# A four-layer decoder on one core: three cross-attentions project queries before context keys, and two memsets in the layer-2 self-attention wait for the first normalised tiles

## The chip, the cores and the metric

The kernel runs on one core of one Trainium2 chip. The metric is the time of one execution on the device in microseconds, as the median of three runs. Six instruction queues work side by side and meet through semaphores: TensorE (PE, whose weight loads are listed as PEld), VectorE (DVE), ScalarE (ACT), GpSimd (POOL) and SyncE (SP), which here only issues transfers.

## What is computed

The reference is a decoder of four layers on `x` of 4 sequences, 512 tokens and 256 features, in float32. Each layer is `x += attention(layernorm(x))`, `x += cross_attention(layernorm(x), ctx)`, `x += ffn(layernorm(x))`, each of a kind of its own. The change touches four of the twelve stages. The three cross-attentions (layers 1, 2 and 3) have one form:

```python
x   = layer_norm(x, ...)              # here ctx, 64 rows a sequence
lat = layer_norm(latents, ...)        # here the 512 tokens
q = lat @ Wq
kv = concatenate([x, lat], axis=1) @ Wkv
k, v = split(kv, 2, axis=-1)
# layers 2 and 3: q and k are scaled to unit (rms or l2) rows, head by head
dots = einsum('bhid,bhjd->bhij', q, k) * scale
out = einsum('bhij,bhjd->bhid', softmax(dots), v) @ Wout
```

There are 16 heads of 64 in layers 1 and 2, and 8 heads of 64 in layer 3; layers 2 and 3 also mask context keys. The self-attention of layer 2 is a masked softmax attention with 16 heads of 16.

## The kernel before

The residual `k.x` stays in SBUF for the whole program (16 tiles of 128 tokens). Each stage is a function with a block of its own, in which each engine's instructions are written out by hand, in order, with semaphore waits. Between two stages all engines meet in a barrier, so a stage's weights are loaded and its first tiles normalised before TensorE has anything to do there. There is no scheduler: the order in the source is the order on each engine.

**Cross-attention** (`latent_attention`, called by `l1_xattn`, `l2_xattn`, `l3_xattn`; `unit` is set for layers 2 and 3). Ahead of the first batch's attention stand these steps:

- SP loads the context rows, small rows, then `Wkv`, `Wq` and the output weights (L2287 to L2293).
- DVE: statistics of the four token tiles of batch 0, two memsets, statistics of the context (L2826, L2829), `batch_scale` of the four token tiles (L2726), the scaled context `cn` (L2834), and for `unit` two operations on the mask. POOL computes the inverse deviations of tokens (L2644, L2647) and of the context (L2685, L2687).
- PE: `turn_batch` twice (L2338, four transposes each, both through bank 7, so the second waits until ACT has taken the first), eight small transposes of the context (L2465), then the projection "units" through the ring of banks 7, 0, 1, 2.
- ACT: `batch_gain` twice (L2534), then the context copied with gain and offset into `ctx2` (twice, L2599) and for `unit` into `ctxT` (L2603).

A unit is one projection of 512 features by two matmuls over the 256 inputs. The first `N0` units are context keys: 8 in layer 1 (256 columns), 4 in layer 2, 2 in layer 3 (512 columns). `NQ` units per batch follow for queries and token keys: 16, 16 and 8. In layer 1 ACT and DVE take turns in copying a unit out. With `unit`, each goes through a pipeline: `project` on PE (L2369), square on ACT, sum over 64 on DVE (L2748), a small scaling with a floor (L2751), the power -0.5 on POOL (L2667), the scaling on DVE (L2758), and `turn_unit` on PE three steps later (L2390). The trace records two matmul passes for each float32 matmul, so a unit is four records. Only when all units of batch 0 are placed does the first score follow (L2493).

**Layer-2 self-attention** (`l2_attn`). At its start DVE makes statistics of four tiles (L2034, L2041), POOL the inverse deviations (L1994, L1996), and then POOL fills `neg_max` and `values_and_ones` with three memsets (L2015, L2016, L2018). DVE scales the four tiles (L2048), PE transposes them (L1807), and the first key and query units follow (L1814). The memsets are first wanted by the first row maximum (`ones_set` 1) and by the first value unit (`ones_set` 3).

## Time and profile before

| | us |
|---|---|
| three runs | 3913.72, 3920.90, 3924.44 |
| median | 3920.9 |
| profiled execution, whole | 3895.01 |
| its span | 3893.3 |

The busy shares of the span are PE 89%, DVE 56%, ACT 39%, POOL 36%. The stages touched start at 605 us (layer-1 cross-attention), 1566 us (layer-2 self-attention), 1946 us (layer-2 cross-attention) and 3125 us (layer-3 cross-attention) of the span. In a timeline a row is a start, a length, the engine, the line, what is written from what, how many instructions, and in brackets how long the engine was idle before and what released it. The granted TensorE clock is 1.00 at 2.4 GHz and 0.50 at 1.2 GHz.

### The profile page before, as it was taken

The numbers are of one execution on the slowest core, as the hardware profiler recorded it, in microseconds if no ns is written. First come the engines' busy times: TensorE is split into PE (matmuls) and PEld (weight loads), VectorE is DVE, ScalarE is ACT, GpSimd is POOL, SyncE is SP. The second block draws the span as 40 slices with busy tenths as digits, with TensorE's granted clock in tenths as the row PEclk, the third lists the DMA queues.
The fourth block names the chain that finished last, engine by engine and source line by source line (L and its number), as shares of the span: only waits on it lengthen the run. The fifth ranks groups of instructions, "written<-read, shape, count | busy, mean of one in ns | idle before, by whom it ended". The sixth has DMA issues, their size and how long they took to land. (4 is left out here: it accounts for less than half of the span.)

```text
span 3893.3 us, 54516 instructions
## 1 busy us (share of the span) xinstructions
PE 3471.5 (89%) x18930; PEld 2243.6 (58%) x18930; DVE 2192.1 (56%) x5349; ACT 1506.5 (39%) x3064; POOL 1392.1 (36%) x1928
## 2 busy tenths in 40 slices
PE   7998897999999978788888999999896979997996
PEld 5675684445555557344444555556794445555996
DVE  6374444646555558666367676765434456665454
ACT  2253102434434265133344444443453134443453
POOL 2141441423223245233244445443423134443412
PEclk9999978999999988899889999999898889997998
DMA  2005001000000000000010000000421000003312
GB/s 101 1 1 125 15 1 46 1 1 1 1 1 1 13 1 1 24 1 1 1 49 1 1 1 1 1 1 1 165 90 60 1 29 1 1 1 112 126 57 83
DMA packets 48720, 108.86 MB, mean 28 GB/s; under 512 B 6660, under 2 KB 32900, under 8 KB 46404
## 3 DMA queue, kind: packets, MB, share of 16 engines
q1 hardware_dynamic: 40964, 84.88, 6.6%
q0 software_dynamic: 7488, 20.49, 1.5%
q8 instruction: 158, 2.59, 0.3%
q14 instruction: 110, 0.90, 0.1%
HBM read 70.67 MB, written 34.68 MB: 27 GB/s over the span
## 5 line engine op out<-in xcount | busy, mean ns | idle before, releaser
L2655 POOL TENSOR_SCALAR probs<-probs,inv_sum 128x512 f32<-128x512 f32 x640 | 438.2, 698 | 997.2 <-DVE inv_sum L2776 996.9
L2618 ACT ACTIVATE probs<-psum_banks,neg_max 128x576 f32<-128x576 f32 x640 | 468.5, 737 | 733.2 <-DVE neg_max L2861 733.2
L2861 DVE TENSOR_REDUCE neg_max<-psum_banks 128x1 f32<-128x576 f32 x640 | 455.0, 752 | 209.4 <-PE psum_banks L2493 202.8
L2493 PE MATMUL psum_banks<-keys_T,queries_T 64*128 64x288 f32 x2560 | 405.7, 436 | 52.5 <-ACT probs L2618 43.2
L2785 DVE COPY probs_T<-psum_banks 128x512 f32<-128x512 f32 x640 | 409.0, 680 | 4.2 <-PE psum_banks L2411 4.2
L2493 PEld LDWEIGHTS psum_banks<-keys_T,queries_T 64*128 64x128 f32 x2560 | 223.8, 189 | 268.8 <-ACT probs L2618 147.7
L2411 PE MATMUL psum_banks<-ident,probs 128*128 128x128 f32 x2560 | 357.6, 284 | 3.3 <-POOL probs L2655 2.4
L2411 PEld LDWEIGHTS psum_banks<-ident,probs 128*128 128x128 f32 x2560 | 281.2, 143 | 129.2 <-POOL probs L2655 75.2
L2443 PE MATMUL psum_banks<-probs_T,values 128*64 128x512 f32 x1280 | 311.3, 608 | 2.2 <-issue 2.2
L4419 PE MATMUL psum_banks<-sorted_T,tile_weights 128*128 128x128 f32 x2208 | 266.9, 278 | 0.0
L4419 PEld LDWEIGHTS psum_banks<-sorted_T,tile_weights 128*128 128x128 f32 x2208 | 259.5, 195 | 0.1
L2857 DVE TENSOR_TENSOR psum_banks<-psum_banks,key_mask 128x128 f32<-128x128 f32 x192 | 57.5, 299 | 273.3 <-PE psum_banks L2493 273.3
L2667 POOL TENSOR_TENSOR square_sum<-square_sum,neg_half 128x8 f32<-128x8 f32 x102 | 167.0, 1639 | 69.8 <-DVE square_sum L2751 68.3
L4318 POOL DMA_INDIRECT expert_outputs<-expert_rows,output_index x92 | 89.7, 975 | 268.6 <-DVE expert_rows L4703 115.8
L4435 PE MATMUL psum_banks<-w_L_experts_down,hidden_T 128*128 x736 | 174.3, 380 | 2.2 <-DVE expert_rows L4703 1.4
L2346 PE MATMUL psum_banks<-w_L_xattn_Wkv,batch_normed_T 128*128 128x512 f32 x320 | 156.3, 612 | 0.0
L2443 PEld LDWEIGHTS psum_banks<-probs_T,values 128*64 128x64 f32 x1280 | 78.9, 137 | 134.0 <-issue 123.2
L4500 ACT COPY tile_weights<-w_L_experts_up 128x1024 f32 (+1 forms) x92 | 135.3, 1472 | 22.9 <-issue 22.9
L4435 PEld LDWEIGHTS psum_banks<-w_L_experts_down,hidden_T 128*128 128x128 f32 x736 | 132.8, 190 | 17.2 <-issue 2.9
L1962 ACT ACTIVATE probs_T<-psum_banks 128x512 f32<-128x512 f32 (+3 forms) x128 | 83.0, 701 | 127.4 <-PE psum_banks L1899 126.5
L2658 POOL TENSOR_TENSOR context_probs<-probs,inv_sum 128x128 f32<-128x128 f32 x320 | 128.7, 402 | 0.0
L2618 ACT ACTIVATION_READ_ACCUMULATOR probs<-psum_banks,neg_max 128x1 f32 x640 | 125.4, 196 | 0.0
(538 smaller groups left out, 6160.1 us busy)
## 6 DMA issues: line engine op xcount, KB each, us to landing
normed<-sorted_rows SPq DMA_DIRECT2D x30, 385.5 KB, 3.4
sorted_rows<-zero_rows SPq DMA_DIRECT2D x8, 1028.0 KB, 16.6
w_L_experts_down<-in_L_experts_down SPq DMA_DIRECT2D x2, 4096.0 KB, 20.4
normed<-expert_outputs SPq DMA_DIRECT2D x8, 1024.0 KB, 6.9
w_L_xattn_Wkv<-in_L_xattn_Wkv SPq DMA_DIRECT2D x2, 2048.0 KB, 8.3
w_L_experts_up<-in_L_experts_up SPq DMA_DIRECT2D x1, 4096.0 KB, 12.2
sorted_rows<-zero_rows SPq DMA_DIRECT2D x4, 899.5 KB, 15.9
x_res<-in_x SPq DMA_DIRECT2D x4, 512.0 KB, 6.7
```

What stands on the lines that cost most here:

```text
L2346: last = pe.matmul(k.ps[:, 7, :], rows, wkv[:, c, W + a * 512:W + (a + 1) * 512], start=c == 0, stop=c == KC - 1)
L2411: last = pe.transpose(k.ps[:, 4 + n % 2, c * P:(c + 1) * P], prob[:, (b * NS + s) % PB, at + c * P:at + (c + 1) * P], k.ident[:, :])
L2443: last = pe.matmul(k.ps[r, 6, :], values[:, b % VB, c, (2 * j + h) * 64:(2 * j + h + 1) * 64], pT[:, q % 2, h, c, :], start=c == 0, stop=F ...
L2493: last = pe.matmul(k.ps[:, 2 * h + a, 0:HALF], qT[r, b % 2, j, t * P:(t + 1) * P], kT[r, j, k0:k0 + HALF], start=True, stop=True)
L2618: act.activation(prob[:, g % PB, h * w:(h + 1) * w].rearrange("p (a n) -> p a n", a=2), k.ps[:, 2 * h:2 * h + 2, 0:HALF], ACT.Exp, bias=nm ...
L2655: pool.tensor_scalar(w, w, inv[:, g % 4, h:h + 1], 1.0, ALU.mult, ALU.mult).then_inc(shared, 1)
L2667: pool.tensor_tensor(ss[:, i % 4, 2, :], ss[:, i % 4, 1, :], k.half[:, 0:8], ALU.pow).then_inc(inverted, 1)
L2785: dve.tensor_copy(pT[:, q % 2, h, :, t * P:(t + 1) * P], k.ps[:, 4 + n % 2, :].rearrange("p (c q) -> p c q", q=P)).then_inc(copied, 1)
L2861: dve.tensor_reduce(nmax[:, g % 4, h:h + 1], k.ps[:, 2 * h:2 * h + 2, 0:HALF], AX.XY, ALU.max, negate=True).then_inc(maxed, 1)
L4419: last = pe.matmul(ps[:, 2 * (n % 2) + part, f * P:(f + 1) * P], wt[:, n % 2, c, part * 512 + f * P:part * 512 + (f + 1) * P], xsT[:, n % ...
L4435: last = pe.matmul(ps[:, 6, 0:D], h[:, n % 2, f * P:(f + 1) * P], w_down[:, f // F, f % F * D:f % F * D + (E - 1) * STEP + D][:, bass.ds(a ...
L4500: act.copy(wt[:, n % 2, :, :], w_up[:, :, 0:(E - 1) * STEP + UP][:, :, bass.ds(at, UP)]).then_inc(weights_copied, 1)
```

## The change

In the three cross-attentions the first four units are now units of batch 0 (`AHEAD` = 4); the `N0` context units follow, and then the rest. The context transposes stand behind the third unit. The second `turn_batch` of batch 0 goes through bank 0, with no wait for ACT between the two. DVE scales the token tiles ahead of the context's statistics, and the context rows behind step 0; the mask operations stand behind step 3. ACT fills `ctxT` (or, in layer 1, the first copy of `ctx2`) at step 3, and the rest of `ctx2` later. SP loads `Wq` first, then the key half of `Wkv` with a semaphore of its own, then the value half. In the layer-2 self-attention POOL waits for the four scaled tiles before its memsets. No operation is dropped or added, apart from one more transfer a stage, since `Wkv` comes in two.

```diff
                 batch_rstd(0)
+                pool.wait_ge(normed, TT)
                 pool.memset(top[:, :, :], 0.0).then_inc(ones_set, 1)
...
+    AHEAD = 4
+    CONTEXT_TURN = 3
+    CONTEXT_COPY = AHEAD + N0 + 1
...
+        def is_context(i):
+            return AHEAD <= i < AHEAD + N0
+
+        def unit_place(i):
+            return (0, i) if i < AHEAD else ((i - N0) // NQ, (i - N0) % NQ)
...
-                sp.dma_start(wkv[:, :, :], wkv.src[:, :, :]).then_inc(kv_loaded, 16)
                 sp.dma_start(wq[:, :, :], wq.src[:, :, :]).then_inc(q_loaded, 16)
+                sp.dma_start(wkv[:, :, 0:W], wkv.src[:, :, 0:W]).then_inc(keys_loaded, 16)
+                sp.dma_start(wkv[:, :, W:2 * W], wkv.src[:, :, W:2 * W]).then_inc(kv_loaded, 16)
...
                 turn_batch(0, 0)
-                pe.wait_ge(norm_moved, 1)
-                turn_batch(0, 1)
+                turn_batch(0, 1, 0)
+                pe.wait_ge(norm_moved, KC)
+                pe.wait_ge(q_loaded, 16)
+                if not unit:
+                    pe.wait_ge(keys_loaded, 16)
+                for i in range(CONTEXT_TURN):
+                    step(i, 0, units_before(1))
                 pe.wait_ge(ctx_normed, B)
...
-                pe.wait_ge(norm_moved, KC)
+                for i in range(CONTEXT_TURN, units_before(1) + 3):
+                    if i == AHEAD:
+                        pe.wait_ge(ctx_ready, KC)
+                        pe.wait_ge(keys_loaded, 16)
+                    step(i, 0, units_before(1))
                 pe.wait_ge(ctx_ready, (3 if unit else 2) * KC)
                 pe.wait_ge(kv_loaded, 16)
-                for i in range(N0):
-                    step(i, 0, units_before(1))
-                pe.wait_ge(q_loaded, 16)
-                for i in range(N0, units_before(1) + 3):
-                    step(i, 0, units_before(1))
...
                 for i in range(units_before(1) + 3):
+                    if i == CONTEXT_TURN:
+                        for c in range(KC):
+                            act.wait_ge(ctx_turned, c + 1)
+                            if unit:
+                                act.activation(ctxT[:, c, :], k.ps[:, 4 + c, 0:B * NC], ACT.Identity,
...
+                            else:
+                                context_rows(c, 0)
+                    if CONTEXT_COPY <= i < CONTEXT_COPY + KC:
+                        if unit:
+                            context_rows(i - CONTEXT_COPY, 0)
+                        context_rows(i - CONTEXT_COPY, 1)
                     step(i, 0, units_before(1))
...
+                for t in range(TT):
+                    batch_scale(0, t)
                 dve.wait_ge(ctx_loaded, 16)
...
-                for t in range(TT):
-                    batch_scale(0, t)
+                step(0, 0, units_before(1))
                 dve.wait_ge(ctx_rstd, 1)
...
+                for i in range(1, AHEAD):
+                    step(i, 0, units_before(1))
```

On PE at the start of the layer-1 cross-attention there stood, from the token transposes on (rows of the program's order, in which a count is of matmuls):

```order
L2338 MATMUL psum_banks<-ident,batch_normed 128x128 x8
L2465 MATMUL psum_banks<-ident,probs_T 128x64 x8
L2377 MATMUL psum_banks<-context_T_twice,w_L_xattn_Wkv 128x256 x16
L2381 MATMUL psum_banks<-batch_normed_T,w_L_xattn_Wq 128x512 x2
L2381 MATMUL psum_banks<-batch_normed_T,w_L_xattn_Wkv 128x512 x2
```

Now there stands, on the same engine and from the same place (line numbers are those of the changed file):

```order
L2349 MATMUL psum_banks<-ident,batch_normed 128x128 x8
L2393 MATMUL psum_banks<-batch_normed_T,w_L_xattn_Wq 128x512 x2
L2393 MATMUL psum_banks<-batch_normed_T,w_L_xattn_Wkv 128x512 x2
L2393 MATMUL psum_banks<-batch_normed_T,w_L_xattn_Wq 128x512 x2
L2482 MATMUL psum_banks<-ident,probs_T 128x64 x8
L2393 MATMUL psum_banks<-batch_normed_T,w_L_xattn_Wkv 128x512 x2
L2389 MATMUL psum_banks<-context_T_twice,w_L_xattn_Wkv 128x256 x16
```

Three units moved ahead of the context transposes, and one more ahead of the context keys.

On DVE at the start of the layer-2 cross-attention there stood (`probs_T` holds the context rows here):

```order
L2823 MEMSET context_values 64x512 x2
L2826 BN_STATS context_stat<-probs_T 64x6 x4
L2829 BN_AGGR context_mv<-context_stat 64x2 x4
L2726 TENSOR_SCALAR batch_normed<-x_res,batch_mv,batch_rstd 128x256 x4
L2834 TENSOR_SCALAR probs_T<-probs_T,context_mv,context_rstd 64x256 x4
L2839 TENSOR_SCALAR key_mask<-w_mask_bf 128x256
L2841 TENSOR_SCALAR key_mask<-key_mask 128x256
L2748 TENSOR_REDUCE square_sum<-squares 128x8
L2751 TENSOR_SCALAR square_sum<-square_sum 128x8
```

Now there stands:

```order
L2848 MEMSET context_values 64x512 x2
L2751 TENSOR_SCALAR batch_normed<-x_res,batch_mv,batch_rstd 128x256 x4
L2853 BN_STATS context_stat<-probs_T 64x6 x4
L2856 BN_AGGR context_mv<-context_stat 64x2 x4
L2773 TENSOR_REDUCE square_sum<-squares 128x8
L2776 TENSOR_SCALAR square_sum<-square_sum 128x8
L2860 TENSOR_SCALAR probs_T<-probs_T,context_mv,context_rstd 64x256 x4
L2773 TENSOR_REDUCE square_sum<-squares 128x8
L2776 TENSOR_SCALAR square_sum<-square_sum 128x8
```

The token tiles are scaled before the context is looked at, and the scaled context moved behind the first unit's square sum.

## Rows read from the trace of the kernel before

**Rows 1.** The page: busy time and share of each engine

```profile
PE 3471.5 (89%) x18930; PEld 2243.6 (58%) x18930; DVE 2192.1 (56%) x5349; ACT 1506.5 (39%) x3064; POOL 1392.1 (36%) x1928
```

**Rows 2.** Timeline, start of the layer-1 cross-attention, all engines

```profile
605.82 0.57 SPq L2291 DMA_DIRECT2D w_L_xattn_Wkv<-in_L_xattn_Wkv  x1
...
607.44 1.01 POOL L2647 TENSOR_TENSOR batch_rstd<-batch_rstd,neg_half 128x4 f32<-128x4 f32 x1
...
608.83 1.40 DVE L2826 BATCH_NORM_STATS2 context_stat<-probs_T 64x6 f32<-64x256 f32 x4 [0.46 <-DMA probs_T<-in_ctx_rows]
...
610.56 1.34 DVE L2726 TENSOR_SCALAR batch_normed<-x_res,batch_mv,batch_rstd 128x256 f32<-128x256 f32 x4
...
611.95 1.11 PE L2338 MATMUL psum_banks<-ident,batch_normed 128*128 128x128 f32 x4 [13.55 <-DVE batch_normed L2726]
...
613.94 1.12 PE L2338 MATMUL psum_banks<-ident,batch_normed 128*128 128x128 f32 x4 [0.87 <-ACT batch_normed_T L2534]
...
614.98 1.11 PE L2465 MATMUL psum_banks<-ident,probs_T 64*128 64x64 f32 x8
...
615.77 1.92 ACT L2599 ACTIVATE context_T_twice<-psum_banks,feature_vectors 128x256 f32<-128x256 f32 x4
...
617.79 9.30 PE L2377 MATMUL psum_banks<-context_T_twice,w_L_xattn_Wkv 128*128 128x256 f32 x32 [1.69 <-issue]
```

**Rows 3.** Transfers in 600 to 640 us: size, us to landing

```profile
w_L_xattn_Wkv<-in_L_xattn_Wkv SPq DMA_DIRECT2D x1, 2048.0 KB, 8.1
```

**Rows 4.** Timeline, start of the layer-2 cross-attention, all engines

```profile
1948.32 0.43 SPq L2291 DMA_DIRECT2D w_L_xattn_Wkv<-in_L_xattn_Wkv  x1
...
1948.93 1.02 POOL L2647 TENSOR_TENSOR batch_rstd<-batch_rstd,neg_half 128x4 f32<-128x4 f32 x1
...
1953.44 1.11 PE L2338 MATMUL psum_banks<-ident,batch_normed 128*128 128x128 f32 x4 [8.92 <-DVE batch_normed L2726]
...
1960.19 8.80 PE L2369 MATMUL psum_banks<-w_L_xattn_Wkv,probs_T 128*128 128x512 f32 x16 [2.61 <-issue]
```

**Rows 5.** Transfers in 1940 to 1975 us: size, us to landing

```profile
w_L_xattn_Wkv<-in_L_xattn_Wkv SPq DMA_DIRECT2D x1, 2048.0 KB, 8.5
```

**Rows 6.** Timeline, start of the layer-3 cross-attention, PE

```profile
3138.49 6.71 PE L2369 MATMUL psum_banks<-w_L_xattn_Wkv,probs_T 128*128 128x512 f32 x8 [2.61 <-issue]
```

**Rows 7.** Timeline, start of the layer-2 self-attention, all engines

```profile
1568.84 1.01 POOL L1996 TENSOR_TENSOR token_rstd<-token_rstd,neg_half 128x4 f32<-128x4 f32 x1
...
1569.80 1.80 POOL L2015 MEMSET neg_max<- 128x2048 f32 x1
1569.96 6.28 DVE L2048 TENSOR_SCALAR batch_normed<-x_res,token_mv,token_rstd 128x256 f32<-128x256 f32 x4 [1.49 <-POOL token_rstd L1996]
...
1576.30 1.97 PE L1807 MATMUL psum_banks<-ident,batch_normed 128*128 128x128 f32 x8 [11.65 <-DVE batch_normed L2048]
...
1579.03 3.75 PE L1814 MATMUL psum_banks<-batch_normed_T,w_L_padded_Wk 128*128 128x512 f32 x4 [0.77 <-ACT batch_normed_T L1951]
```

**Rows 8.** Durations of single lines: ns min/median/max, first and last start

```profile
L2048 DVE TENSOR_SCALAR batch_normed<-x_res,token_mv,token_rstd x16: 396/406/5237, 1570.0 to 1767.6; 128x256 f32<-128x256 f32 x16
...
L2751 DVE TENSOR_SCALAR square_sum<-square_sum x102: 171/171/206, 1965.3 to 3453.6; 128x8 f32<-128x8 f32 x102
...
L2685 POOL TENSOR_SCALAR context_rstd<-context_mv x3: 1230/1232/1232, 610.7 to 3130.5; 64x4 f32<-64x4 f32 x3
...
L2644 POOL TENSOR_SCALAR batch_rstd<-batch_mv x12: 194/194/195, 607.2 to 3409.7; 128x4 f32<-128x4 f32 x12
```

**Rows 9.** Windows: stretch, its length, busy time of each engine, granted clock, DMA

```profile
618.00:622.10 4.10, 4.10 (x10) 3.25 (x11) 0.42 (x1) 0.37 (x1) 0.00 (x0) 0.50 0.01 2
...
1566.00:1946.00 380.00, 314.61 (x2144) 157.15 (x2144) 218.50 (x392) 116.42 (x184) 109.58 (x283) 0.89 0.02 7
...
1576.30:1584.70 8.40, 7.63 (x15) 4.09 (x16) 0.00 (x0) 1.86 (x3) 0.00 (x0) 0.50 0.00 0
...
1960.10:1963.60 3.50, 3.41 (x4) 1.50 (x5) 0.00 (x0) 0.00 (x0) 0.00 (x0) 0.50 0.14 56
```

More of the change, by code:

```diff
@@ L2332, in bank_free, with turn_batch @@
                                 pe.wait_ge(ctx_value_moved, b * A + A)
-                def turn_batch(b, c):
+                def turn_batch(b, c, bank=7):
                     if c == 0:
@@ L2337, in turn_batch @@
                     for t in range(TT):
-                        last = pe.transpose(k.ps[:, 7, t * P:(t + 1) * P], xr[:, t, c * P:(c + 1) * P], k.ident[:, :])
+                        last = pe.transpose(k.ps[:, bank, t * P:(t + 1) * P], xr[:, t, c * P:(c + 1) * P], k.ident[:, :])
                     last.then_inc(norm_turned, 1)
@@ L2375, in project @@
                     for c in range(KC):
[L2376 to L2377 removed]
+                        if is_context(i):
+                            j = i - AHEAD
+                            last = pe.matmul(k.ps[:, unit_bank(i), 0:B * NC], wkv[:, c, j * P:(j + 1) * P],
                                              ctx2[:, c, :, 0, :], start=c == 0, stop=c == KC - 1)
                         else:
[L2380 removed]
+                            j, w = unit_place(i)[1] // 2, (wkv if i % 2 else wq)
                             last = pe.matmul(k.ps[:, unit_bank(i), :], w[:, c, j * P:(j + 1) * P], xT[:, c, :],
@@ L2533, in batch_gain @@
                     act.wait_ge(norm_turned, KC * b + c + 1)
-                    act.activation(xT[:, c, :], k.ps[:, 7, :], ACT.Identity, bias=k.vec(pre + lb)[:, c:c + 1],
+                    bank = 0 if b == 0 and c == 1 else 7
+                    act.activation(xT[:, c, :], k.ps[:, bank, :], ACT.Identity, bias=k.vec(pre + lb)[:, c:c + 1],
                                    scale=k.vec(pre + lg)[:, c:c + 1]).then_inc(norm_moved, 1)
@@ L2540, in project @@
                     act.wait_ge(made, i + 1)
-                    if i < N0:
-                        act.copy(kc[:, i, :, :].rearrange("p b n -> p (b n)"),
+                    if is_context(i):
+                        act.copy(kc[:, i - AHEAD, :, :].rearrange("p b n -> p (b n)"),
                                  k.ps[:, unit_bank(i), 0:B * NC]).then_inc(act_moved, 1)
                     else:
-                        b, j = (i - N0) // NQ, (i - N0) % NQ // 2
+                        b, j = unit_place(i)[0], unit_place(i)[1] // 2
                         act.mul(qT[:, b % 2, j, :], k.ps[:, unit_bank(i), :], 0.125).then_inc(act_moved, 1)
@@ L2563, in step, with context_rows @@
                                 gain).then_inc(moved, 1)
+                def context_rows(c, i):
+                    act.activation(ctx2[:, c, :, i, :], k.ps[:, 4 + c, 0:B * NC].rearrange(
+                        "p (b n) -> p b n", b=B), ACT.Identity, bias=k.vec(pre + cb)[:, c:c + 1],
+                        scale=k.vec(pre + cg)[:, c:c + 1]).then_inc(ctx_ready, 1)
                 def copy_ctx(b, j):
@@ L2595, in _ @@
                     batch_gain(0, c)
-                for c in range(KC):
-                    act.wait_ge(ctx_turned, c + 1)
-                    for i in range(2):
-                        act.activation(ctx2[:, c, :, i, :], k.ps[:, 4 + c, 0:B * NC].rearrange(
-                            "p (b n) -> p b n", b=B), ACT.Identity, bias=k.vec(pre + cb)[:, c:c + 1],
-                            scale=k.vec(pre + cg)[:, c:c + 1]).then_inc(ctx_ready, 1)
-                    if unit:
-                        act.activation(ctxT[:, c, :], k.ps[:, 4 + c, 0:B * NC], ACT.Identity,
-                                       bias=k.vec(pre + cb)[:, c:c + 1],
-                                       scale=k.vec(pre + cg)[:, c:c + 1]).then_inc(ctx_ready, 1)
-                for i in range(units_before(1) + 3):
+                for i in range(units_before(1) + 3):
+                    if i == CONTEXT_TURN:
[3 more added lines that the diff above has]
+                                act.activation(ctxT[:, c, :], k.ps[:, 4 + c, 0:B * NC], ACT.Identity,
+                                               bias=k.vec(pre + cb)[:, c:c + 1],
+                                               scale=k.vec(pre + cg)[:, c:c + 1]).then_inc(ctx_ready, 1)
+                            else:
[4 more added lines that the diff above has]
+                        context_rows(i - CONTEXT_COPY, 1)
                     step(i, 0, units_before(1))
@@ L2764, in place @@
                     if unit:
-                        dve.wait_ge(moved, N0)
+                        dve.wait_ge(moved, AHEAD + N0)
                     else:
-                        dve.wait_ge(act_moved, N0 // 2)
-                        dve.wait_ge(dve_moved, N0 // 2)
+                        dve.wait_ge(act_moved, (AHEAD + N0) // 2)
+                        dve.wait_ge(dve_moved, (AHEAD + N0) // 2)
                     if b:
@@ L2842, in _ @@
                     dve.wait_ge(mask_made, 2)
-                for i in range(units_before(1) + 1):
+                for i in range(AHEAD, units_before(1) + 1):
                     step(i, 0, units_before(1))
```

19 lines of the change are left out of this document (8 added, 11 removed).

## The prediction

> **What bounds the kernel now.** The page comes first: PE is busy 89% of the span, DVE 56%, and no other engine is near [rows 1]. Such a share is an average over twelve stages, and the change touches only the first microseconds of four of them, so I read the timelines of those starts. Because a barrier stands ahead of each stage, nothing can overlap its start, and a microsecond saved there ends the stage a microsecond earlier, provided that PE's queue is what the stage then runs on. In these starts PE is the engine that waits. Before the token transposes it is idle for 13.55 us in layer 1, 8.92 us in the layer-2 cross-attention and 11.65 us in the layer-2 self-attention, each time released by DVE's scaled tiles [rows 2, 4, 7]; part of this is the end of the stage before. It is idle again, 1.69, 2.61 and 2.61 us, before the first context unit [rows 2, 4, 6].
>
> What the reader is to see in [rows 2] is the order of causes. POOL has the tokens' inverse deviation at 607.44 + 1.01 = 608.45. DVE could scale the tiles then, but its queue has the context's statistics first (608.83), and it scales at 610.56. PE turns tile half 0 at 611.95, waits 0.87 us for ACT to empty bank 7, turns the second half, then the context (1.11 us). Now ACT needs four copies of the context (1.92 us from 615.77), and only after them does the first unit start, at 617.79. The queries need none of the context's work.
>
> **The token scaling, moved ahead.** In the self-attention the scales start 0.11 us after POOL's power has ended (1569.85 to 1569.96) [rows 7]; so in layer 1 they start at 608.56, take their 1.34 us [rows 2], and PE begins at 609.95 instead of 611.95. In the layer-2 cross-attention the power ends at 1949.95 [rows 4], so PE begins at 1951.45 instead of 1953.44. The context statistics then run beside PE's transposes.
>
> **Two banks for the two turns.** Two turns of 1.11 us back to back and then ACT's last copy, of the size of the 0.87 us wait: 2.22 + 0.87 = 3.1 us. PE is ready for the first unit at 613.05 in layer 1, 1954.55 in layer 2.
>
> **The loads.** Layer 1 needs `Wq` and the key half of `Wkv`, together the same 2 MB that `Wkv` had alone. Those were issued at 605.82 and landed 8.1 us later [rows 2, 3], so at 613.9; with one more issue in between I take 614.0. The weights are thus the last to arrive there, by 0.9 us. In layer 2 the first unit needs only `Wq`, 1 MB. The 2 MB of `Wkv`, from 1948.32, took 8.5 us [rows 4, 5]: half the size lands between half of that (1952.6) and all of it (1956.8). I take 1954.55, where PE is ready, since the middle of the two is 1954.7; the late end would cost 2.2 us. The same holds in layer 3 with half the bytes. The key half in layers 2 and 3 has four units of time to land, and the value half is wanted only after all units: nothing.
>
> **The units.** The first one starts at 614.0 instead of 617.79: 3.8 us. In layer 2 it starts at 1954.55 instead of 1960.19: 5.6 us. Layer 3 shows the same 2.61 us of idle before its first context unit [rows 6] and the same code ahead of it; I take 5.5. From this goes what was ahead of the units and now stands among them: eight context transposes, 1.11 us at the half clock, 0.55 at the full clock that I expect behind the third unit. Results: **3.2, 5.1 and 5.0 us**. The number of units, their columns and the ring of banks are as before. ACT's copies of the context for the values move into the stream of units: 1.92 us for four, so 0.96 for each of two steps. A unit is 8.80 us for four, half of it at the lower clock [rows 4], some 1.8 us of PE, plus a turn; ACT has a square and a gain in that time and room for about 1 us. I cost them at 0, and at 0.5 us a stage if ACT is late. The mask's two DVE operations move likewise: 0, since PE turns a unit three steps after it projects it.
>
> **The memsets.** In [rows 7] DVE starts four scales at 1569.96, and they end at 1576.24. One of the sixteen scales of this stage took 5237 ns, the median is 406 [rows 8]; in the cross-attention, beside transfers at full load but no memset, four take 1.34 us. The one long scale lies under POOL's memsets, which began at 1569.80. With POOL waiting, the scales end at 1571.30 and PE starts at 1571.36 instead of 1576.30: **4.9 us**. What is queued behind POOL's new wait is the memsets alone. They need about 5.5 us, so end near 1577. The key unit, moved from 1579.03 to about 1574.1, the query and the first score come before the first row maximum, and before any value unit; before, these stood past 1584 [rows 9]. So the wait itself costs 0. If the memsets blocked another DVE operation in their new place, at most the 4.9 us would be given back. Only 1 MB of weights is wanted for key and query, and the larger 2 MB of layer 1 landed in 8.1 us, so they are there.
>
> **Sum.** 3.2 + 4.9 + 5.1 + 5.0 = **18.2 us**. The profiled span of 3893.3 us would become 3875.1. The profiled execution lies 26 us under the median of the three runs, which scatter by 10.7 us, so I apply the difference to the median: 3920.9 - 18.2 = **3902.7**.
>
> **A rule against the change.** In layers 2 and 3 the four context scales on DVE (SBUF to SBUF) now stand right behind the square sum that releases POOL's power, some 1.6 us long. Rows show the conflict in two directions: the memset held a scale for 5.2 us, and `context_rstd` on POOL took 1230 ns, against 194 for its kin on the tokens, while DVE scaled tiles [rows 8]. The third row speaks against it for the power: the small scaling on DVE, which comes next to powers, never took over 206 ns. The Trainium skill, page "SBUF — State Buffer", section "Who interferes with whom", says that the one of VectorE (in a two-port mode) and GpSimd that issues first holds the shared ports for its whole instruction and the other is fully blocked. By it the context scales could come a whole power later.
>
> **Rivals.** (1) *The clock eats half of it.* All four starts run at 1.2 GHz: PEclk is 0.50 up to 622.1, 1584.7 and 1963.6 [rows 9]. If the clock rose at these same moments however early PE starts, the time gained would be worked at half rate: lost are half of 3.8, of 5.6, of 5.5 and of 4.9, about 10 us, and the result is 3912.8, within 0.3%. For it: the clock is no engine's queue. Against it: each rise came 3.4 to 5.7 us after PE had begun to work without a gap (617.79, 1960.19, 1579.03), whatever the stage; so it follows the work, and moves with it. (2) *The port is held.* A unit at half rate is 3.4 us, its square and sum I estimate at 1.7, the power at 1.6, then the four scales at 1.4: the context is ready 8.1 us after the first unit's start. PE arrives at 3.4 + 2 x 1.75 = 6.9 us if the clock rises early: a wait of 1.2 us, twice, so 3905.1. (3) *The memset is not the cause*, and the scales stay slow: 13.3 us, 3907.6. One long row and its start beside the memset speak against it. (4) *Slower.* The clock also falls and rises inside the layer-2 self-attention, 0.89 on average over 380 us, so 84 us at half rate [rows 9], where PE, DVE and POOL hand work to each other. All of this is now met at other moments. Each microsecond more at half rate costs up to half of one, so the gain is gone from 36 us more on; 48 us more would give 3927. Nothing in the change lengthens PE's gaps there, and three runs of one program differ by 10.7 us in all, so this is a tail.
>
> **How the numbers follow.** Forecast with all four terms 0.70, the clock 0.18, the port 0.05, the memset 0.04, slower 0.03. A measurement tells about 0.3% (11.8 us) from no change, so all but the clock and the tail would be faster by more. The forecast lies only 6 us beyond that bound, and the medians scatter by some microseconds each; I take faster 0.74, same 0.23, slower 0.03. The range goes down to 3891 (the clock rises earlier relative to the first unit, and scatter of the runs) and up to 3913, the clock rival.
>
> **What would show it.** In the changed profile PE's first token transpose comes 2.0 us earlier from each cross-attention's first DVE statistics, with no gap between the two turns; the first unit of layer 1 starts about 8.2 us after the issue of its first weights, waiting for a transfer. No scale in the self-attention is over 0.5 us. The first score comes 3, 5 and 5 us sooner in its stage. It is wrong if the rise of the clock stays where it was, if PE has a gap before the context transposes, or if the row maxima wait for a memset.

## The result, and the profile after

| | before, us | after, us |
|---|---|---|
| median of the runs | 3920.9 (5 runs, 3913.72 to 3924.44) | 3901.12 (5 runs, 3896.46 to 3907.86) |
| profiled execution, whole | 3895.01 | 3901.12 |
| its span | 3893.3 | 3899.4 |

The ratio is 0.9949, with a 95% interval of 0.9934 to 0.9964: 19.8 us faster, where 18.2 were forecast (3902.7). A second comparison, on a later occasion, gave 3900.14 against 3921.65 us, ratio 0.9942 (0.9929 to 0.9955). So the kernel is faster by about 0.5%.

The two profiled spans alone would say the opposite: 6.1 us slower. Whoever compares profiles has to look at the stages. Stage lengths, from the first transfer that SP issues in a stage to that of the next, in us. The third column is a second profile of the kernel before, taken beside the second comparison:

| stage | before | before, again | after |
|---|---|---|---|
| layer-1 cross-attention | 730.6 | 730.7 | 730.2 |
| layer-1 feed-forward (untouched) | 230.8 | 224.7 | 228.5 |
| layer-2 self-attention | 380.1 | 385.4 | 372.5 |
| layer-2 cross-attention | 782.4 | 783.0 | 779.1 |
| layer-2 experts and layer-3 self-attention (untouched) | 396.0 | 412.8 | 412.7 |
| layer-3 cross-attention | 439.9 | 440.2 | 432.7 |
| layer-3 experts (untouched) | 304.3 | 314.4 | 315.3 |

The four touched stages together went from 2333.0 to 2314.5: 18.5 us. What hides it are two stretches of untouched code, which in the first profile of before happened to be 16.7 and 11.0 us shorter than after, and which the same kernel shows long in its second profile. A second profile of the changed kernel has them long too (413.0 and 315.0), so only the first profile of before is short. Whether that is the execution, the chip or the occasion is not shown: 12 runs of this kernel on one chip lie within 17 us (3913.64 to 3930.48). By the two second profiles the four touched stages went from 2339.3 to 2317.5, 21.8 us. The windows of the first stretch say so, before, before again, and after (columns: stretch, its length, busy time and count of PE, PEld, DVE, ACT, POOL, granted clock, DMA share, GB/s):

```profile
2729.00:3125.00 396.00, 336.43 (x1744) 254.00 (x1744) 156.46 (x398) 135.98 (x223) 128.00 (x120) 0.86 0.23 78
```

```profile
2730.70:3143.50 412.80, 343.16 (x1744) 257.61 (x1744) 155.82 (x398) 135.67 (x223) 128.90 (x120) 0.85 0.22 74
```

```profile
2714.50:3127.20 412.70, 342.56 (x1744) 257.45 (x1744) 155.79 (x398) 135.66 (x223) 128.77 (x120) 0.85 0.22 74
```

The same 1744 matmuls; before again and after agree to 0.1 us. Of the 16.8 us more in the second profile of before, 6.7 are longer PE busy time, and the rest is PE idle time. Most of that stands ahead of the expert matmuls of this line, 0.7 us in the first profile and 10.6 in the second (columns: busy, mean ns, idle before):

```profile
L4435 PE MATMUL psum_banks<-w_L_experts_down,hidden_T 128*128 x368 | 87.1, 380 | 0.7 <-DVE expert_rows L4698 0.7
```

```profile
L4435 PE MATMUL psum_banks<-w_L_experts_down,hidden_T 128*128 x368 | 91.0, 392 | 10.6 <-DVE expert_rows L4698 9.8 <-issue 0.8
```

**The starts, after.** The page: the shares of [rows 1] are unchanged.

```profile
PE 3474.5 (89%) x18930; PEld 2246.4 (58%) x18930; DVE 2184.8 (56%) x5349; ACT 1506.1 (39%) x3064; POOL 1389.5 (36%) x1928
```

Timeline of the layer-1 cross-attention's start, all engines, which answers to [rows 2] (columns as there; the stage begins at 604.20, before at 605.2):

```profile
604.82 0.57 SPq L2301 DMA_DIRECT2D w_L_xattn_Wq<-in_L_xattn_Wq  x1
...
606.43 1.01 POOL L2672 TENSOR_TENSOR batch_rstd<-batch_rstd,neg_half 128x4 f32<-128x4 f32 x1
...
607.48 1.38 DVE L2751 TENSOR_SCALAR batch_normed<-x_res,batch_mv,batch_rstd 128x256 f32<-128x256 f32 x4
...
608.91 1.97 PE L2349 MATMUL psum_banks<-ident,batch_normed 128*128 128x128 f32 x8 [11.52 <-DVE batch_normed L2751]
610.07 1.63 ACT L2551 ACTIVATE batch_normed_T<-psum_banks,feature_vectors 128x512 f32<-128x512 f32 x2 [16.46 <-PE psum_banks L2349]
...
613.66 2.90 PE L2393 MATMUL psum_banks<-batch_normed_T,w_L_xattn_Wq 128*128 128x512 f32 x3 [2.78 <-DMA w_L_xattn_Wkv<-in_L_xattn_Wkv]
```

The scales follow POOL's power at once, the two turns are one row of eight without a gap, and the first unit waits 2.78 us for a transfer, the key half of `Wkv`. The layer-2 cross-attention (stage start 1935.40), against [rows 4]:

```profile
1940.12 1.97 PE L2349 MATMUL psum_banks<-ident,batch_normed 128*128 128x128 f32 x8 [6.89 <-DVE batch_normed L2751]
...
1943.95 7.85 PE L2380 MATMUL psum_banks<-w_L_xattn_Wq,batch_normed_T 128*128 128x512 f32 x12 [1.86 <-DMA w_L_xattn_Wq<-in_L_xattn_Wq]
...
1949.17 1.37 DVE L2860 TENSOR_SCALAR probs_T<-probs_T,context_mv,context_rstd 64x256 f32<-64x256 f32 x4
1949.34 1.74 POOL L2692 TENSOR_TENSOR square_sum<-square_sum,neg_half 128x8 f32<-128x8 f32 x1 [6.19 <-DVE square_sum L2776]
...
1951.73 0.71 PE L2482 MATMUL psum_banks<-ident,probs_T 64*128 64x64 f32 x8
```

And in the layer-3 cross-attention (stage start 3127.2), against [rows 6]:

```profile
3134.72 7.67 PE L2380 MATMUL psum_banks<-w_L_xattn_Wq,batch_normed_T 128*128 128x512 f32 x11 [0.87 <-ACT batch_normed_T L2551]
```

The layer-2 self-attention (stage start 1562.89), against [rows 7]:

```profile
1566.24 1.38 DVE L2049 TENSOR_SCALAR batch_normed<-x_res,token_mv,token_rstd 128x256 f32<-128x256 f32 x4 [1.49 <-POOL token_rstd L1996]
...
1567.68 1.97 PE L1807 MATMUL psum_banks<-ident,batch_normed 128*128 128x128 f32 x8 [6.75 <-DVE batch_normed L2049]
1567.68 1.80 POOL L2016 MEMSET neg_max<- 128x2048 f32 x1 [1.55 <-DVE batch_normed L2049]
...
1569.43 3.51 POOL L2017 MEMSET values_and_ones<- 128x4096 f32 x1
...
1570.41 3.45 PE L1814 MATMUL psum_banks<-batch_normed_T,w_L_padded_Wk 128*128 128x512 f32 x4 [0.77 <-ACT batch_normed_T L1951]
```

Durations of single lines (ns, min/median/max), against [rows 8]:

```profile
L2049 DVE TENSOR_SCALAR batch_normed<-x_res,token_mv,token_rstd x16: 404/406/412, 1566.2 to 1756.3; 128x256 f32<-128x256 f32 x16
```

```profile
L2710 POOL TENSOR_SCALAR context_rstd<-context_mv x3: 187/188/188, 610.7 to 3133.6; 64x4 f32<-64x4 f32 x3
```

No scale is over 412 ns, where one took 5237. And POOL's small operation for the context went from 1230 ns to 188: DVE now scales tokens before it.

Windows around the rise of the clock, in the order of the stages, against [rows 9]:

```profile
613.60:617.70 4.10, 4.04 (x5) 1.85 (x6) 0.00 (x0) 0.25 (x1) 0.00 (x0) 0.50 1.01 421
617.70:622.00 4.30, 4.30 (x17) 2.01 (x16) 0.69 (x1) 1.26 (x3) 0.00 (x0) 1.00 0.01 4
1570.40:1573.40 3.00, 2.98 (x4) 1.45 (x5) 0.00 (x0) 0.00 (x0) 2.86 (x2) 0.50 0.02 10
...
1943.90:1948.90 5.00, 4.95 (x6) 2.19 (x7) 0.53 (x1) 0.60 (x1) 0.00 (x0) 0.50 1.02 389
1948.90:1951.70 2.80, 2.80 (x7) 0.95 (x5) 2.52 (x9) 0.60 (x1) 1.74 (x1) 1.00 0.54 228
3134.70:3140.20 5.50, 5.48 (x7) 2.38 (x8) 0.99 (x3) 0.60 (x1) 0.26 (x2) 0.50 0.44 176
```

From the stage's start the clock rose at 17.0, 18.1, 16.9 and 19.5 us before and at 13.5, 10.5, 13.5 and 13.0 us after. It moved with the work.

### The profile page after: what moved, and what is told of

Same layout as the page of the kernel before. It is cut to its first block and busy times, and to the rows that moved or that the text cites. A ratio compares the mean times of both kernels' runs of the same rounds, so it can differ in the third digit from the quotient of the medians.

```text
span 3899.4 us, 54521 instructions
## 1 busy us (share of the span) xinstructions
PE 3474.5 (89%) x18930; PEld 2246.4 (58%) x18930; DVE 2184.8 (56%) x5349; ACT 1506.1 (39%) x3064; POOL 1389.5 (36%) x1928
## 5 line engine op out<-in xcount | busy, mean ns | idle before, releaser
L4463 PE MATMUL psum_banks<-w_L_experts_down,hidden_T 128*128 x736 | 180.0, 388 | 17.3 <-DVE expert_rows L4726 11.7
```

The costliest lines, as they stand in the source:

```text
L4463: last = pe.matmul(ps[:, 6, 0:D], h[:, n % 2, f * P:(f + 1) * P], w_down[:, f // F, f % F * D:f % F * D + (E - 1) * STEP + D][:, bass.ds(a ...
```

## The experiments

Eight of the twelve stages are as they were, and two of them vary by more than the change is worth. So most kernels here hold only the four touched stages, one after the other; the other eight and the filling of the expert rows are left out. They ran on three chips, with the kernel before beside them: at 3898.5 us for `four_before`, `four_after`, `four_memset` and `four_warm`, at 3893.8 for `four_context_first`, `four_scale_late`, `four_keys_load_first` and `four_one_memset`, and at 3921.7 for `four_crosses` and the whole kernels. `four_before` and `four_after` ran on the first of them alone, so the medians of the last five are compared across chips. So each verdict is read from the stage lengths of the profile too. These are one execution each: with the same code up to there, first scores still differ by up to 1.5 us (51.9 and 50.8 in layer 1, 13.6 to 15.1 in the self-attention). "First score" is the time from a stage's start to its first score matmul.

| us | median | L1 cross | L2 self | L2 cross | L3 cross | first scores |
|---|---|---|---|---|---|---|
| `four_before` | 2355.61 | 731.4 | 385.4 | 782.7 | 436.4 | 51.9, 19.6, 62.9, 40.9 |
| `four_after` | 2333.47 | 728.9 | 372.5 | 778.8 | 432.7 | 47.7, 13.8, 59.1, 37.2 |
| `four_memset` | 2346.66 | 730.2 | 375.1 | 782.3 | 439.1 | 50.8, 15.1, 62.9, 40.8 |
| `four_crosses` | 2342.10 | 728.1 | 381.9 | 778.8 | 432.7 | 48.6, 19.2, 59.0, 37.1 |
| `four_context_first` | 2342.40 | 728.6 | 374.9 | 782.5 | 435.9 | 49.1, 15.0, 61.6, 40.4 |
| `four_scale_late` | 2340.00 | 729.6 | 375.6 | 778.6 | 436.9 | 48.5, 13.6, 60.6, 38.4 |
| `four_keys_load_first` | 2348.51 | 731.3 | 372.2 | 785.5 | 437.2 | 50.2, 13.6, 65.7, 38.8 |
| `four_one_memset` | 2339.41 | 729.1 | 379.3 | 779.1 | 432.5 | 47.9, 16.2, 59.9, 37.0 |
| `four_warm` | 2329.62 | 728.8 | 375.8 | 775.1 | 429.4 | 47.8, 13.1, 57.3, 33.8 |

**The four stages alone, before and after.** The same code, with the list of stages cut.

> The kernel before with only the four touched stages left in (three cross-attentions and the layer-2 self-attention); the other eight stages and the filling of rows for the experts are left out. It is the base for the other kernels of this size. Sum of the four stages in the profile of before: 730.6 + 380.1 + 782.4 + 439.9 = 2333 us, and some 15 us for loading and storing: 2350. Theory (the start of each stage is all that changed): the runs of this kernel agree within about 5 us, since the expert stages, which I hold for the source of most of the scatter, are gone. Rival (the scatter is the clock's): they scatter by 10 us as the whole kernel does.

Its runs lie within 6.3 us (2350.14 to 2356.46), between what the theory and its rival gave.

> The changed kernel with the same four stages alone. Theory: the whole gain lies in these stages and in nothing else, 18 us (17 to 20) less than the same four of before. Rival (a part of the measured 19.8 us is luck, or lies in stages that were not changed): 10 to 14 us less.

22.1 us by the medians, 23.0 by the stages: the gain is in the touched stages, whatever the experts do. It is more than the 17 to 20 us expected. At the first scores 17.5 us are gained, and another 7.1 behind the first score of the self-attention (365.8 to 358.7 us), which are taken up below; 1.7 are lost behind that of layer 1.

**The memset wait alone**, on the kernel before:

```diff
                 batch_rstd(0)
+                pool.wait_ge(normed, TT)
                 pool.memset(top[:, :, :], 0.0).then_inc(ones_set, 1)
```

> The four stages of before with one edit: the memsets of the layer-2 self-attention wait for the four scaled tiles. Theory: the scales take 1.4 us instead of 6.3, PE begins 4.9 us earlier, and the clock rises with it: 4.9 to 6.2 us less than the four stages of before. Rival (memsets were not what held the scales, or they hold something else later): 0 to 2 us.

8.95 us by the median, where 4.9 to 6.2 were expected. The first score comes 4.5 us sooner. The remaining 5.8 us of the stage's 10.3 came behind the first score (365.8 to 360.1 us), where nothing was edited, and there the trace shows 64.9 us at the low clock instead of 78.5. The first profile of before had 360.2 us there with no wait for the memsets, so these 5.8 us are not shown to come from the wait.

**The three cross-attentions alone**, the changed kernel without that one line:

```diff
                 batch_rstd(0)
-                pool.wait_ge(normed, TT)
                 pool.memset(top[:, :, :], 0.0).then_inc(ones_set, 1)
```

> The four touched stages alone (the other eight are left out), with the change to the three cross-attentions and without the wait ahead of the memsets. If the two parts add up: 22.1 us of gain less 9.0 of the wait alone leave 13.1, so 2342.5 us, 9 us above the four stages with the whole change; by the first scores alone (5.9 us for the memsets) 2339.4. The self-attention's first score stands at about 19.7 us behind its start, the cross-attentions' as with the whole change (47.7, 59.1, 37.2).

13.5 us under `four_before`; with the 8.95 of the other part 22.5, against 22.1 for both. The parts add up, with the caution that this run is from another chip than the other three; by the stage lengths it is 14.4 and 9.2 us against 23.0 for both. Of the 14.4, 3.1 lie behind the first score of the self-attention (365.8 to 362.7 us), whose code is that of before. Its timeline has the old row again, and PE behind it:

```profile
742.97 6.28 DVE L2048 TENSOR_SCALAR batch_normed<-x_res,token_mv,token_rstd 128x256 f32<-128x256 f32 x4 [1.51 <-POOL token_rstd L1996]
```

```profile
749.30 1.97 PE L1807 MATMUL psum_banks<-ident,batch_normed 128*128 128x128 f32 x8 [11.36 <-DVE batch_normed L2048]
```

**One memset ahead of the wait.** Is it the memset's length that DVE pays? Here only the 1.8 us one stays beside the scales, and the 3.5 us one waits:

```diff
-                pool.wait_ge(normed, TT)
                 pool.memset(top[:, :, :], 0.0).then_inc(ones_set, 1)
+                pool.wait_ge(normed, TT)
```

> The four stages of after with the shorter of the memsets (1.8 us) put back ahead of POOL's wait, the longer ones behind it. Theory (a POOL memset holds a DVE scale for as long as it runs): the first of the four scales takes about 1.8 us in place of 0.4, and PE begins 1.5 us later in this stage, 6.3 instead of 4.8 us after its start. Rival (it needs a memset that is already long under way, or several in a row): no change.

```profile
743.70 1.80 POOL L2015 MEMSET neg_max<- 128x2048 f32 x1
743.86 2.75 DVE L2049 TENSOR_SCALAR batch_normed<-x_res,token_mv,token_rstd 128x256 f32<-128x256 f32 x4 [1.51 <-POOL token_rstd L1996]
...
746.67 3.51 POOL L2017 MEMSET values_and_ones<- 128x4096 f32 x1 [1.17 <-DVE batch_normed L2049]
```

The four scales take 2.75 us: 1.38 with no memset beside them, 6.28 with two. The first of the four took 1.79 us, where 1.8 was expected. The differences, 1.37 and 4.90, are close to what is left of the memsets when the scales begin (743.86 is 0.16 into a memset of 1.80, so 1.64 remain; of 5.25 us for both, 5.1 remain). So DVE stands still while POOL fills, and that is shown by three lengths. The median, 5.9 us above `four_after` (on another chip), is more than this 1.4: the first score is 2.4 late, since the clock rose later, and the rest of the stage took 4.5 us more, at 71.7 us of low clock against 61.4. The expectation missed that.

**The context first again**: the order of units of before, with the early scales and the two banks kept.

```diff
-    AHEAD = 4
-    CONTEXT_TURN = 3
+    AHEAD = 0
+    CONTEXT_TURN = 0
...
-                step(0, 0, units_before(1))
                 dve.wait_ge(ctx_rstd, 1)
```

> The four stages of after with the order of units undone: the context units come first again and wait for the context's copies; the scales ahead of the context statistics, the two banks, the split loads and the memset's wait stay. Theory (queries need nothing of the context, and that is worth more than the early scales): the first unit starts near 11.7 us after the stage's start instead of 8.8, 7.7 and 7.6, less 0.55 us for the context transposes that leave the stream; 3 us more in layer 1 and 3.5 in each of the others, some 9 us more than the four stages of after. Rival (the early scales and the second bank carry the gain): 0 to 3 us more.

8.9 us by the median, where some 9 were expected. That agreement is partly luck: by the stage lengths 2.4 of 9.0 us lie in the self-attention, whose code is that of `four_after`. In its layer-2 cross-attention PE waits for the context twice:

```profile
1124.17 1.08 PE L2482 MATMUL psum_banks<-ident,probs_T 64*128 64x64 f32 x8 [2.60 <-DVE probs_T L2859]
...
1125.94 9.24 PE L2380 MATMUL psum_banks<-w_L_xattn_Wkv,probs_T 128*128 128x512 f32 x14 [0.68 <-ACT probs_T L2623]
```

The first unit is 11.05 us behind the stage's start, 7.7 with the queries first. By the lengths of the three stages together, 1950.5 us before, 1940.4 after and 1947.0 here, the order of units carries 6.6 us of the cross-attentions' 10.1.

**The token scales late again**, behind the context's statistics:

```diff
-                for t in range(TT):
-                    batch_scale(0, t)
                 dve.wait_ge(ctx_loaded, 16)
...
                     dve.bn_aggr(cmv[0:NC, t, :], cstat[0:NC, t, :]).then_inc(ctx_aggr, 1)
+                for t in range(TT):
+                    batch_scale(0, t)
                 step(0, 0, units_before(1))
```

> The four stages of after with DVE's order undone: the token scales stand behind the context's statistics again. PE's first transpose comes 2.0 us later in each cross-attention. Theory (in layers 1 and 2 a part of this is hidden, since the weights come last): the first unit starts 1 us later in layer 1, 1 to 2 in layer 2, 2 in layer 3; together 4 to 5 us more. Rival (the whole 2.0 us counts three times): 6 us.

```profile
1120.77 1.40 DVE L2851 BATCH_NORM_STATS2 context_stat<-probs_T 64x6 f32<-64x256 f32 x4 [0.84 <-DMA probs_T<-in_ctx_rows]
...
1122.49 1.34 DVE L2751 TENSOR_SCALAR batch_normed<-x_res,batch_mv,batch_rstd 128x256 f32<-128x256 f32 x4
1122.66 1.23 POOL L2710 TENSOR_SCALAR context_rstd<-context_mv 64x4 f32<-64x4 f32 x1 [2.65 <-DVE context_mv L2854]
1123.89 1.97 PE L2349 MATMUL psum_banks<-ident,batch_normed 128*128 128x128 f32 x8 [9.16 <-DVE batch_normed L2751]
```

The turns are 2.4 us later in the stage (7.1 against 4.7). In the two later cross-attentions the first score loses 1.6 and 1.2 us, in layer 1 0.8. The median loses 6.5, where 4 to 5 were expected. The stages also move behind their first scores: 3.3 us are lost in the unedited self-attention (68.3 us of low clock) and 3.0 in layer 3, and 1.8 are won in the layer-2 cross-attention, whose stage is no longer than with the early scales (778.6 against 778.8). So the early scales are worth 3.6 us at the first scores; more is not shown. The 1.23 us on POOL are back too.

**`Wq` loaded last**, behind both halves of `Wkv`:

```diff
-                sp.dma_start(wq[:, :, :], wq.src[:, :, :]).then_inc(q_loaded, 16)
                 sp.dma_start(wkv[:, :, 0:W], wkv.src[:, :, 0:W]).then_inc(keys_loaded, 16)
                 sp.dma_start(wkv[:, :, W:2 * W], wkv.src[:, :, W:2 * W]).then_inc(kv_loaded, 16)
+                sp.dma_start(wq[:, :, :], wq.src[:, :, :]).then_inc(q_loaded, 16)
```

> The four stages of after with the order of loads undone: key half, value half, and then Wq; all else stays. Theory (the first unit waits for its weights already, so any megabyte put ahead of them is paid): the first unit starts 2.4 us later in layer 1 (3 MB instead of 2 ahead), 4 us later in layer 2 (3 MB instead of 1), 1.5 us in layer 3; together 8 us more. Rival (loads were there in time): 0 to 2 us.

```profile
1129.28 1.19 PE L2380 MATMUL psum_banks<-w_L_xattn_Wq,batch_normed_T 128*128 128x512 f32 x1 [7.58 <-DMA w_L_xattn_Wq<-in_L_xattn_Wq]
```

15.0 us by the median, 13.3 by the stages, where 8 were expected. The first unit of the layer-2 cross-attention starts 14.26 us into its stage, later than before the change (13.5). I had under-priced the transfer: `Wq`, third of four in the queue, landed 11.2 us after its issue; first in the queue it took 5.9 in `four_after` and 6.8 in the whole kernel. The three cross-attentions together take 1954.0 us, 1950.5 before the change and 1940.4 in `four_after`; 2.9 us of the loss against `four_after` lie behind the first score of layer 3. Their three first scores add up to 154.7 us, against 155.7 before and 144.0 in `four_after`: without the new order of loads, nearly all that the other parts bring to them is gone.

**A warm engine.** If the four starts run at the half clock because PE is idle, work that nobody needs should raise it earlier. 22 transposes of the identity into a bank that nobody reads stand ahead of the turns, 6 behind them in the cross-attentions:

```diff
+                for _ in range(22):
+                    pe.transpose(k.ps[:, 3, 0:P], k.ident[:, :], k.ident[:, :])
                 turn_batch(0, 0)
                 turn_batch(0, 1, 0)
+                for _ in range(6):
+                    pe.transpose(k.ps[:, 3, 0:P], k.ident[:, :], k.ident[:, :])
```

> The four stages of after, with transposes of the identity matrix into a bank that nobody reads: 22 ahead of the first token transposes of each stage, 6 more between those and the first unit of the cross-attentions. They only keep PE at work where it waits. Theory (the rise of the clock follows PE's work, and each start of after still runs 8 to 10 us of its work at half rate): the clock is up before the first unit, 2 to 4 us less in each stage, 8 to 14 us less than the four stages of after. Rival (the rise is tied to the moment and not to the work): no gain, or 1 to 3 us more where the extra transposes delay the real ones.

```profile
1116.03 4.22 PE L2474 MATMUL psum_banks<-ident 128*128 128x128 f32 x22 [2.08 <-PEq L45]
1120.70 1.09 PE L2351 MATMUL psum_banks<-ident,batch_normed 128*128 128x128 f32 x8 [0.45 <-DVE batch_normed L2757]
...
1124.43 1.96 PE L2382 MATMUL psum_banks<-w_L_xattn_Wq,batch_normed_T 128*128 128x512 f32 x4 [1.98 <-DMA w_L_xattn_Wq<-in_L_xattn_Wq]
```

The turns take 1.09 us instead of 1.97, so the clock does follow PE's work. But the turns being early helps little in this stage: in the last row PE waits 1.98 us for `Wq` all the same. The first scores come 0, 0.7, 1.8 and 3.4 us sooner, 5.8 in all; another 1.9 us is gained behind the first score of layer 2's cross-attention, and 4.0 are lost in the self-attention's rest (71.7 us of low clock against 61.4). 3.9 us stay by the medians, where 8 to 14 were expected, and the runs of the two kernels overlap (2325.14 to 2333.67 and 2329.94 to 2334.98). The rival, that the rise is tied to a moment, is refuted by the turns.

**Whole kernels, on one chip.**

> The kernel before, all twelve stages, again, for the profile of the untouched stages. If the two long expert stages vary from execution to execution by themselves (396 and 304 us in the profile of before, 413 and 315 in that of after, with the same instructions), this profile shows lengths other than 396 and 304, nearer to 410 and 315, and a span above 3893 us. If their length hangs on the change, it shows 396 and 304 again.

> The changed kernel, all twelve stages, again. My theory (the four starts give the whole gain, the eight untouched stages only scatter): 18 to 22 us under the kernel before on this chip, so a ratio near 0.995, the same as in the first measurement, although the level may be another. In the profile the first units stand 7.5 to 9.5 us behind the first load of each cross-attention. The rival (the gain on record is partly luck of the untouched expert stages) expects a difference outside 15 to 25 us.

> The changed kernel with all twelve stages and, in the four starts, 22 transposes of the identity into a bank nobody reads ahead of the token turns, and in the cross-attentions 6 more behind them. With the four stages alone this brought 3.9 us: 9 us at the first scores, 4 us given back in the self-attention's rest. My theory: the same here, 3 to 5 us under the changed kernel. If the give-back is chance of the clock, up to 9; if the noise of the expert stages covers it, nothing that can be told from 0.

(The 9 us at the first scores that the last one takes from `four_warm` is a slip of mine; it is 5.8, as above.) Before 3919.89 us (12 runs; ratio to the other runs of the same kernel 0.9996, 0.9987 to 1.0004); after 3900.14, which is 19.8 us less, or 21.5 under the median of all 17 runs of before (3921.65): 18 to 22 were expected; after with the warm engine 3893.49, ratio to before 0.9926 (0.9913 to 0.9939). Its interval overlaps that of after (0.9929 to 0.9955), and its own profile (of its highest time, 3902.53) shows only 1.1 us at the first scores against the second profile of after. Its four touched stages together are no shorter (2318.8 against 2317.5 us). In layer 1 the clock had fallen again before the first unit. In layer 3 it held:

```profile
3137.78 1.09 PE L2351 MATMUL psum_banks<-ident,batch_normed 128*128 128x128 f32 x8 [2.09 <-DVE batch_normed L2757]
```

So this version may beat both, by 6.6 us over after if the medians are taken as they are, but the runs don't settle that.

## Why the prediction was right, point by point

The form was right: four starts, each worth some microseconds, which go straight to the end. The sum was 18.2 at the first scores and 17.3 in the trace. Two of its terms were too large, by 2.8 us together, and two too small, by 1.9; that the sum comes so near is in part luck. The stages gained 18.5 us, since behind the first scores 2.0 us were lost in layer 1 and 3.2 won in the other three.

| first score, us into the stage | before | after | gained | forecast |
|---|---|---|---|---|
| layer-1 cross-attention | 51.01 | 48.57 | 2.4 | 3.2 |
| layer-2 self-attention | 19.91 | 13.69 | 6.2 | 4.9 |
| layer-2 cross-attention | 62.88 | 59.80 | 3.1 | 5.1 |
| layer-3 cross-attention | 42.71 | 37.11 | 5.6 | 5.0 |

**Token scaling and two banks: right.** PE turns at 4.7 us into each cross-attention, 6.75 before: the 2.0 us forecast. The turns back to back take 1.97 us, I had 2.22.

**Loads: right in kind, low in size.** In layer 1 the first unit was to wait for its weights and does. It starts 8.84 us after the first weight issue, 8.2 was forecast, so 3.1 us are gained at the unit instead of 3.8. In layer 2 I put `Wq` at the moment PE is ready. The transfers of that start, after, against [rows 5]:

```profile
w_L_xattn_Wkv<-in_L_xattn_Wkv SPq DMA_DIRECT2D x2, 1024.0 KB, 9.9
w_L_xattn_Wq<-in_L_xattn_Wq SPq DMA_DIRECT2D x1, 1024.0 KB, 6.8
```

6.8 us for half of the bytes that took 8.5: nearer to the late end of my bounds (4.3 to 8.5) than to the middle. PE waits 1.86 us, of which ACT's copy would have been 0.87. The first unit gains 4.95 us, not 5.6. In layer 3 `Wq` is in time, the wait is ACT's 0.87, and the unit gains 5.9.

**The clock: right to follow the work, not priced.** I let the units start earlier at unchanged speed, and I had read the time from first unit to rise, 3.4 to 5.7 us, in three starts only; in layer 3 it was 6.1. From the first unit to the rise PE ran at half rate for 3.4 us in layer 2 before and for 5.0 after, and in the self-attention for 5.7 before and 3.0 after. Half of the difference is 0.8 us lost and 1.3 gained. With the transposes (0.71 us, I had 0.55) the layer-2 cross-attention comes to 4.95 - 0.8 - 0.7 = 3.4 against 3.1 measured; the self-attention to 4.9 + 1.3 = 6.2 against 6.2. Layer 3 comes to 5.9 - 0.7 + 0.3 = 5.5 against 5.6 (6.1 us at half rate before, 5.4 after). In the four-stage kernels, where the clock of before rose 2.8 us earlier in layer 3 (16.7 us into the stage instead of 19.5), that term is only 3.7. So the sizes hang on where the clock rises as well as on the work that was moved.

**The memsets: right.** The first unit came 4.9 us sooner in its stage (12.42 to 7.52), as computed, and neither the row maxima nor the values waited for the memsets. `four_one_memset` shows the mechanism at a second length, `four_crosses` its return.

**What I did not price: the way behind the first score.** In the layer-1 cross-attention 2.0 of the 2.4 us are gone by the stage's end. At the boundary of two batches PE stops for 2.45 us, before and after; the stretch behind it had the full clock before and half of it after:

```profile
822.25:824.70 2.45, 0.00 (x1) 0.00 (x1) 1.44 (x3) 1.55 (x4) 0.00 (x0) 1.00 0.00 0
825.95:829.35 3.40, 3.40 (x18) 2.23 (x20) 2.69 (x5) 2.18 (x6) 1.30 (x3) 1.00 0.00 0
```

```profile
818.80:821.24 2.44, 0.00 (x0) 0.00 (x0) 1.44 (x3) 1.55 (x4) 0.00 (x0) 1.00 0.00 0
822.50:825.90 3.40, 3.40 (x11) 2.36 (x12) 2.69 (x5) 1.55 (x4) 1.30 (x3) 0.50 0.00 0
```

Of three such boundaries the clock fell at two before, at three after. It goes with the new order, though not strictly: all five profiles with the context first show two falls, and eight of the nine with the queries first show three. The ninth is `four_crosses`, which runs the same instructions up to there as `four_after`. So some 1.6 to 2.0 us of layer 1's gain must be expected to go again; what decides it stays open.

In the self-attention the time behind the first score differs for one and the same kernel: 360.2 us with 65.0 us of low clock in the first profile of before, 365.9 with 78.5 in the second; after, 358.8 with 61.6, and 361.5 with 68.3 in the second. That is 0.4 us per us of low clock, the price that the slower rival assumed at half. The untouched feed-forward of layer 1 shows the same: 224.7 us with 58.0 at the low clock, 228.5 with 68.3, 230.8 with 71.7. In the self-attention it was paid in the change's favour in all comparisons of before and after here, but against `four_after` the later start of `four_one_memset` and the earlier one of `four_warm` both cost 4 us. What sets the low time is not shown.

**The rivals.** (1) The clock's rise stayed where it was: refuted, it moved by 3.4 to 7.6 us. (Half of 19.8 us is 9.9, so its price would have been 3912.6, not 3912.8.) (2) The port held by POOL's power: refuted. DVE scaled the context in 1.37 us while the power ran, the power took 1.74 us instead of 1.64, and the context transposes at 1951.73 have no idle time ahead of them. The rule of the Trainium skill (page "SBUF — State Buffer", section "Who interferes with whom"), by which one of the two is fully blocked, fits the memset and the 1230 ns, and does not fit this pair, where the measurement decides: the scales began 0.17 us before the power, took their usual time, and the power lost 0.1 us. The rival needs the other order, a power that is under way when a VectorE operation comes. The trace has that too. The second to fourth of those scales began 0.15, 0.48 and 0.80 us into the power and took 0.40 us each. And the two mask operations start inside a power of 1.64 us:

```profile
1955.99 1.64 POOL L2692 TENSOR_TENSOR square_sum<-square_sum,neg_half 128x8 f32<-128x8 f32 x1 [0.89 <-DVE square_sum L2776]
...
1956.43 0.28 DVE L2867 TENSOR_SCALAR key_mask<-w_mask_bf 128x256 f32<-128x256 int32 x1
...
1956.75 0.29 DVE L2869 TENSOR_SCALAR key_mask<-key_mask 128x256 f32<-128x256 f32 x1
```

Before the change they took the same 0.28 and 0.29 us with no power beside them. What sets the power apart from the memset is not shown. (3) The memset is not the cause: refuted by three lengths. (4) Slower: the price per us of low clock was about right (0.4), but the low time fell.

## What to carry to other kernels

At a stage's start, put in PE's queue first what needs the fewest predecessors, and put its weights first in the transfer queue too: the first without the second is worth little (`four_keys_load_first`). A fill on GpSimd beside VectorE's scaling of tiles in SBUF cost VectorE the rest of the fill here (1.4 and 4.9 us), so let it wait until VectorE's urgent work is done. And compare stage by stage: two untouched stretches differ by 27 us between two profiles of one kernel, more than the whole change.

## What was not expected of the hardware

- The rest of a stage can take 5.7 us more or less in two executions of one kernel (365.9 and 360.2 us), with 13.5 us more or less at the low clock, with no change in the code ahead of it.
- 1 MB took 6.8 us from issue to landing as the first weight in the queue of the layer-2 start, 5.4 us in layer 1, 11.2 us as the third (`four_keys_load_first`); 2 MB as the first weight had taken 8.1 and 8.5. Half the bytes is far from half the time.
- Dummy matmuls raised the granted clock for the token turns (1.09 us for eight instead of 1.97), but in layer 1 it fell again in the wait for weights that followed; in the whole kernel that left 1.1 us at the first scores of the profiled execution.
- The median of the kernel before was 3920.9, 3898.5, 3893.8 and 3921.7 us on four occasions, 0.7% apart, while the ratios measured side by side repeated within 0.1% (0.9949 and 0.9942).
